# Attention scores from float32 queries and keys, four heads side by side in 32-row groups, in place of bf16 part sums over 96 rows

## What is computed

```python
mod = (silu(c) @ wmod)                     # six rows of 256 per batch: sa, ca, ga, sb, cb, gb
h = layernorm(x) * (1 + ca) + sa
q, k, v = (h @ Wq.T), (h @ Wk.T), (h @ Wv.T)      # 16 heads of 16 dimensions
q, k = rope(q), rope(k)
scores = einsum('bhqd,bhkd->bhqk', q, k) * 16**-0.5     # causal
attn = softmax(scores)
x = x + ga * ((attn @ v) @ Wo.T)
h = layernorm(x) * (1 + cb) + sb
x = x + gb * soft_moe(h)    # 8 experts of 128 slots: dispatch and combine softmax, gelu
```

## Time and profile before

| what | value |
|---|---|
| median of 3 runs | 3296.63 us (3295.2 to 3301.05) |
| the profiled execution: its own time, its span | 3297.0 us, 3295.2 us |
| TensorE matmul busy | 3071.7 us (93% of the span) |
| VectorE busy | 2252.1 us (68%) |
| ScalarE busy | 1763.6 us (54%) |
| GpSimd busy | 329.8 us (10%) |
| attention of batch 0 (first to last weighing) | from 162.6 us to 607 us |

### The profile page before, as it was taken

The page is one execution under the profiler, slowest core; times in us unless marked ns, Lnnn a source line. Parts: engine busy times, 40 slices in busy tenths (PEclk is TensorE's granted clock), DMA queues, the critical chain, the costliest instruction groups (busy, mean ns, idle before and its releaser), DMA issues.

```text
span 3295.2 us, 45435 instructions
## 1 busy us (share of the span) xinstructions
PE 3071.7 (93%) x17679; PEld 1544.8 (47%) x17679; DVE 2252.1 (68%) x4403; ACT 1763.6 (54%) x3199; POOL 329.8 (10%) x193
## 2 busy tenths in 40 slices
PE   5799999999889999998989999999997999999899
PEld 2433334447553333453854333344575433334468
DVE  4788887562678888756368888856546888885632
ACT  2366666564236666645514666654540566665560
POOL 3200000210400000111130000012122000002200
PEclk9799999999999999999999999999999999999999
DMA  4322201015502220002542202000443220100052
GB/s 129 99 40 40 40 2 39 14 52 197 149 20 40 40 40 27 20 7 95 190 119 46 39 9 40 27 20 7 151 163 103 40 41 11 31 27 27 9 179 81
DMA packets 123555, 201.89 MB, mean 61 GB/s; under 512 B 10094, under 2 KB 106996, under 8 KB 120232
## 3 DMA queue, kind: packets, MB, share of 16 engines
q1 hardware_dynamic: 110820, 148.58, 13.9%
q10 hardware_dynamic: 12520, 50.40, 8.2%
HBM read 156.01 MB, written 42.16 MB: 60 GB/s over the span
## 4 chain that ended last, share of the span: by engine, by line
PE 74%; DVE 17%; ACT 4%; issue 2%; POOL 1%; DMA 1%; ACTq 0%; SPq 0%; DVEq 0%; POOLq 0%
PE ps L694 14%; DVE pm L1269 12%; PE ps L674 10%; PE ps L614 9%; PE ps L795 7%; PE ps L850 7%; PE ps L627 6%; PE ps L881 3%; PE ps L870 3%; PE ps L574 2%; PE ps L738 2%; PE ps L659 2%; PE ps L678 1%; PE ps L808 1%; PE ps L603 1%
## 5 line engine op out<-in xcount | busy, mean ns | idle before, releaser
L1269 DVE TENSOR_REDUCE pm<-ps 128x1 f32<-128x512 f32 (+4 forms) x2560 | 1376.9, 602 | 273.6 <-PE ps L614 181.9
L983 ACT ACTIVATE R<-ps 128x512 f32<-128x512 f32 (+1 forms) x2240 | 1175.5, 593 | 603.0 <-PE ps L674 412.1
L674 PE MATMUL ps<-R 99*128 99x512 bf16 (+3 forms) x2560 | 827.9, 349 | 10.7 <-ACT R L983 6.0
L614 PE MATMUL ps<-R 96*128 96x512 bf16 x1536 | 578.6, 387 | 46.2 <-DVE pm L1269 40.7
L694 PE MATMUL ps<-R 128*17 128x512 f32 (+3 forms) x5120 | 528.9, 531 | 0.0
L614 PEld LDWEIGHTS ps<-R 96*128 96x128 bf16 x1536 | 147.3, 97 | 446.4 <-DVE pm L1269 372.0
L674 PEld LDWEIGHTS ps<-R 99*128 99x128 bf16 x2560 | 241.4, 97 | 146.0 <-ACT R L983 64.1
L694 PEld LDWEIGHTS ps<-R 128*17 128x17 f32 x5120 | 117.8, 96 | 280.1 <-issue 168.3
L850 PE MATMUL ps<-R 128*128 128x512 f32 x512 | 231.7, 610 | 14.0 <-ACT R L1050 13.9
L627 PE MATMUL ps<-R 128*128 128x257 f32 x1024 | 237.4, 388 | 4.1 <-ACT R L934 3.6
L795 PE MATMUL ps<-snT,R 128*128 128x512 f32 x512 | 230.1, 593 | 0.0
(11 more groups left out here) (151 smaller groups left out, 3321.7 us busy)
## 6 DMA issues: line engine op xcount, KB each, us to landing
R<-in_L_ffn_w_dram SPq DMA_DIRECT2D x64, 1024.0 KB, 5.8
R<-q_parts ACTq DMA_DIRECT2D x12, 768.0 KB
R<-k_parts ACTq DMA_DIRECT2D x12, 768.0 KB
R<-in_L_attn_x_dram SPq DMA_DIRECT2D x16, 512.0 KB, 8.4
q_parts<-R SPq DMA_DIRECT2D x16, 512.0 KB, 3.6
k_parts<-R SPq DMA_DIRECT2D x16, 512.0 KB, 3.4
R<-in_L_attn_x_dram SPq DMA_DIRECT2D x4, 2048.0 KB, 8.3
x_park<-R SPq DMA_DIRECT2D x16, 512.0 KB, 2.6
```

What stands on the lines that cost most here:

```text
L614: last = mm(ps[:, bank, :], qt(4 * c + r), kt(4 * kc, 4), start=True, stop=True)
L674: last = mm(bank[:, i * w:(i + 1) * w], kst[g % 2][0:BROWS, h0 + i, j * P:(j + 1) * P], qst[g % 2][0:BROWS, h0 + i, (c + 1) * CH - w:(c + ...
L983: A(Eb[s % ESLOTS][:, h0:h0 + n, 0:w], ps[:, u % NST, 0:n * w].rearrange("p (n w) -> p n w", n=n), ACT.Exp, scale=SCALE).then_inc(s_ex, 1)
L1269: mx = lambda o, i: V.tensor_reduce(o, i, AX.X, ALU.max)
```

## The change

Queries and keys stay float32. After the rotation they are parked as they are, 16 rows each, and `load_group` brings each head of a group to its own 32 partitions: head h has its 16 rows at 32h, and row 32h+16 holds ones for keys and the negated maximum for queries. All four groups have their own place in SBUF (`kg`, `qg`). A score matmul runs over 17 rows, a matmul of maxima over 16, in the 32-row group of its head, in float32. The three-part splitting on ScalarE, VectorE and GpSimd goes, as do the four instructions that split the negated maxima; `nrow` has two buffers.

The narrow tiles change: the last two tiles of a chunk (256 and 128 columns) form one step, with one unit per head; in a step at the diagonal the mask matmuls of two units (all 128 rows, 128 or 256 columns) follow behind the second of them. A chunk has 4c+3 steps; a batch has 144 steps and 576 units. The blocks of maxima are "diag", "near" (two matmuls of 256 columns), "edge" (two of 128) and "full", in number 592 as before, and they go round the heads in the order 2, 3, 0, 1 in place of all blocks of one head first. Steps are weighed 4 units behind instead of 3.

```diff
 def steps_of_chunk(k):
-    return 4 * (k % NC) + 4
+    c = k % NC
+    return [(j,) for j in range(4 * c + 2)] + [(4 * c + 2, 4 * c + 3)]
...
+UNITS = [(s, h) for s in range(NSTEP) for h in range(HG)]
...
+    blocks = [("diag", 0, 0), ("near", 0, 0), ("edge", 0, 0)]
+    blocks += [("full", r, kc) for kc in range(c) for r in range(4)]
+    for kind, r, kc in blocks:
+        for h in (2, 3, 0, 1):
+            yield k, h, kind, r, kc
...
-WEIGH_BEHIND, EVAC_BEHIND, TURN_BEHIND, GATHER_BEHIND = 3, 5, 8, 9
+WEIGH_BEHIND, EVAC_BEHIND, TURN_BEHIND, GATHER_BEHIND = 4, 5, 8, 9
...
-        kst = [view(R1, 8192 * i, 4096, bf16).rearrange("p (h t) -> p h t", h=HG) for i in range(2)]
-        qst = [view(R1, 8192 * i + 4096, 4096, bf16).rearrange("p (h t) -> p h t", h=HG) for i in range(2)]
+        kg = [view(R1, 4096 * g, 2048) for g in range(NG)]
+        qg = [view(R1, 4096 * g + 2048, 2048) for g in range(NG)]
...
+            for h in range(HG):
+                rows = slice(32 * h, 32 * h + HD)
+                eng.dma_start(kg[g][rows, tokens], k_park[:, HG * g + h, tokens]).then_inc(loaded, 16)
+                eng.dma_start(qg[g][rows, tokens], q_park[:, HG * g + h, tokens]).then_inc(loaded, 16)
+            eng.dma_start(kg[g][HD:P:32, tokens], ones_park[:, tokens]).then_inc(loaded, 16)
...
                 def qt(i):
-                    return qst[g % 2][0:KROWS, h, i * P:(i + 1) * P]
+                    return qg[g][32 * h:32 * h + KROWS, i * P:(i + 1) * P]
...
                 elif kind == "diag":
-                    mm(ps[:, bank, :], identb[:, :], maskb[:, :, :].rearrange("p r t -> p (r t)"),
-                       start=True, stop=True)
+                    mm(ps[:, bank, :], identb[:, :], maskq[:, :, :].rearrange("p r t -> p (r t)"),
+                       start=True, stop=True, skip_group_check=True)
...
+                elif kind == "near":
+                    mm(ps[:, bank, 0:2 * P], qt(4 * c + 2), kt(4 * c, 2), start=True, stop=True)
+                    last = mm(ps[:, bank, 2 * P:4 * P], qt(4 * c + 3), kt(4 * c, 2), start=True, stop=True)
+                elif kind == "edge":
                     mm(ps[:, bank, 0:P], qt(4 * c + 1), kt(4 * c, 1), start=True, stop=True)
-                    last = mm(ps[:, bank, P:4 * P], qt(4 * c + 3), kt(4 * c, 3), start=True, stop=True)
-                elif kind == "even":
-                    last = mm(ps[:, bank, 0:2 * P], qt(4 * c + 2), kt(4 * c, 2), start=True, stop=True)
+                    last = mm(ps[:, bank, P:2 * P], qt(4 * c + 3), kt(4 * c + 2, 1), start=True, stop=True)
...
                 def score_unit(u):
...
+                    rows = slice(32 * h, 32 * h + BROWS)
+                    for j, at, w in tiles_of_step(s):
+                        last = mm(ps[:, u % NST, at:at + w], kg[g][rows, j * P:(j + 1) * P],
+                                  qg[g][rows, (c + 1) * CH - w:(c + 1) * CH], start=at == 0, stop=True, skip_group_check=True)
+                    if not diagonal(s):
+                        last.then_inc(s_st, 1)
+                    elif h % 2:
+                        mask_units(u - 1, u)
+
+                def mask_units(*pair):
+                    for u in pair:
+                        s, h = UNITS[u]
+                        n = len(tiles_of_step(s))
+                        bank = ps[:, u % NST, :].rearrange("p (n w) -> p n w", n=2)
+                        mm(bank[:, 0:n, 0:P], identb[:, :], maskk[:, 0:n, :],
+                           start=False, stop=True, skip_group_check=True).then_inc(s_st, 1)
...
-            def parts(b, i):
-
-                qk = i % 2
-                act.wait_ge(s_rr, b * QU + i + 1)
-                nc.scalar.copy(rope_part[set_of(b, i)][qk], rope_out[set_of(b, i)]).then_inc(s_p0, 1)
-                act.wait_ge(s_r2, b * QU + i + 1)
-                nc.scalar.copy(rope_part[set_of(b, i)][1 - qk], rope_out[set_of(b, i)]).then_inc(s_p1, 1)
...
-            def remainder(b, i):
-                dve.wait_ge(s_p0, b * QU + i + 1)
-                V.tensor_tensor(out=rope_out[set_of(b, i)], in0=rope_out[set_of(b, i)], in1=rope_part[set_of(b, i)][i % 2],
-                                op=ALU.subtract).then_inc(s_r2, 1)
...
-                V.tensor_reduce(negm[:, :, :], pm[:, k % 2, :, :, 0:2 + k % NC], AX.X, ALU.max, negate=True).then_inc(s_own_nm, 1)
...
-                V.tensor_tensor(out=negp[:, :, 2, :], in0=negr[:, :, :], in1=negp[:, :, 1, :], op=ALU.subtract).then_inc(s_nm, 1)
+                V.tensor_reduce(negm[:, :, :], pm[:, k % 2, :, :, 0:3 + k % NC], AX.X, ALU.max, negate=True).then_inc(s_nm, 1)
```

More of the change, by code:

```diff
@@ L40, in steps_of_chunk, with tiles_of_step, step_width @@
 def steps_of_chunk(k):
-    return 4 * (k % NC) + 4
-STEPS = [(k, j) for k in range(NK) for j in range(steps_of_chunk(k))]
+    c = k % NC
+    return [(j,) for j in range(4 * c + 2)] + [(4 * c + 2, 4 * c + 3)]
+STEPS = [(k, js) for k in range(NK) for js in steps_of_chunk(k)]
 NSTEP = len(STEPS)
-FIRST_STEP = [STEPS.index((k, 0)) for k in range(NK)]
-LAST_STEP = [FIRST_STEP[k] + steps_of_chunk(k) - 1 for k in range(NK)]
-def diagonal(s):
[L53 to L62, removed]
+FIRST_STEP = [[k for k, js in STEPS].index(c) for c in range(NK)]
+LAST_STEP = [FIRST_STEP[k] + len(steps_of_chunk(k)) - 1 for k in range(NK)]
+def tiles_of_step(s):
+    k, js = STEPS[s]
+    out, at = [], 0
+    for j in js:
+        w = CH - max(j - 4 * (k % NC), 0) * P
+        out.append((j, at, w))
+        at += w
+    return out
+def step_width(s):
+    return sum(w for j, at, w in tiles_of_step(s))
+def diagonal(s):
+    k, js = STEPS[s]
+    return js[0] >= 4 * (k % NC)
+UNITS = [(s, h) for s in range(NSTEP) for h in range(HG)]
 SU = len(UNITS)
-FIRST_UNIT = [[u[0] for u in UNITS].index(s) for s in range(NSTEP)]
-LAST_UNIT = [FIRST_UNIT[s + 1] - 1 if s + 1 < NSTEP else SU - 1 for s in range(NSTEP)]
+FIRST_UNIT = [HG * s for s in range(NSTEP)]
+LAST_UNIT = [HG * s + HG - 1 for s in range(NSTEP)]
 def max_units_of_chunk(k):
     c = k % NC
[L71 to L77, removed]
+    blocks = [("diag", 0, 0), ("near", 0, 0), ("edge", 0, 0)]
[3 more added lines that the diff above has]
+            yield k, h, kind, r, kc
 ROWS_BEHIND = 4
@@ L139 @@
 LAST_UNIT_OF_CHUNK = [LAST_UNIT[LAST_STEP[k]] for k in range(NK)]
-WEIGH_AFTER = after_units([LAST_UNIT[s | 1] for s in range(NSTEP)], WEIGH_BEHIND)
+WEIGHED = [pair for k in range(NK) for pair in
+           [(s, s + 1) for s in range(FIRST_STEP[k], LAST_STEP[k], 2)] + [(LAST_STEP[k],)]]
+WEIGH_AFTER = after_units([LAST_UNIT[pair[-1]] for pair in WEIGHED], WEIGH_BEHIND)
 EVAC_AFTER = after_units(LAST_UNIT_OF_CHUNK, EVAC_BEHIND)
@@ L335, in adaln_block @@
         s_rr = sem("roped_ready")
[L336 to L339, removed]
[L340 removed]
+        s_pk = [sem(f"roped_parked{i}") for i in range(RSETS)]
         s_ldf = [sem(f"first_group_loaded{c}") for c in range(NC)]
@@ L670, in score_unit @@
                     if u >= NST:
                         pe.wait_ge(s_ex, b * SU + (u + 1 - NST))
-                    bank = ps[:, u % NST, :]
-                    for i in range(n):
-                        last = mm(bank[:, i * w:(i + 1) * w], kst[g % 2][0:BROWS, h0 + i, j * P:(j + 1) * P],
-                                  qst[g % 2][0:BROWS, h0 + i, (c + 1) * CH - w:(c + 1) * CH],
-                                  start=i == 0, stop=True, skip_group_check=True)
-                    if diagonal(s) >= 0:
-                        last = mm(bank[:, 0:n * w].rearrange("p (n w) -> p n w", n=n)[:, :, 0:P], identb[:, :],
-                                  maskTb[:, 0:n, :], start=False, stop=True, skip_group_check=True)
@@ L779, in _ @@
                         beside(BESIDE_AT.index(u))
-                for s in range(NSTEP):
-                    if LAST_UNIT[s | 1] + WEIGH_BEHIND >= SU:
-                        weigh(s)
+                for pair in WEIGHED:
+                    if LAST_UNIT[pair[-1]] + WEIGH_BEHIND >= SU:
+                        for s in pair:
+                            weigh(s)
                 def logits(n):
@@ L947, in _ @@
                 modulated(0, c)
-            for i in range(QU):
-                parts(0, i)
             act.wait_ge(s_pt, 3)
@@ L1093, in _ @@
                         modulated(b + 1, c)
[L1094 to L1102 removed]
+                for c in range(NC):
+                    store(c)
         @block.gpsimd
```

187 lines of the change are left out of this document (61 added, 126 removed).

## The result

| | before | after |
|---|---|---|
| median of 4 runs | 3298.23 us (3295.2 to 3301.05) | 5818.98 us (5810.76 to 5820.14) |
| ratio of after to before, 95% interval | | 1.7638 [1.7607, 1.7668] |
| span of the profiled execution | 3295.2 us | 5808.9 us |
| mean granted clock of TensorE over the span | 0.981 | 0.689 |
| forecast | | 3790 us, range 3500 to 4180 |

What follows compares the result with a forecast made beforehand. Attention was taken as bound by TensorE's stream, VectorE close behind, and after the change by latency of the bank rings. Attention +464, maxima outside +70 and savings -39 gave +495 on 3297.0 us: 3790 us, range 3500 to 4180.

Steps and rivals of the forecast that it cites:

- a rival of 3%: Attention: no overlap of row groups, 16.1 us a pair, about 6150 us; a waits-lowered clock between 4480 and 6150; chance 3%.
- 464: All four attentions: 116 us more per batch, a group of heads taking 143 us instead of 112.2.
- The "diag" blocks: Attention: mask 0.2 us, switching 0.2 and lost overlap, about 0.6 us per block, 2.0 us per chunk.
- the bank turn: Attention: a bank is free again after 1.71 us (scores) or 1.80 us (maxima), so one per 0.57 or 0.60 us.
- a full pair: Attention, weighing to weighing: 7.15 us against 6.18 seen before, bounds 6.6 and 8.0; 12 pairs per group.
- the pair at the diagonal: Attention, once per chunk: masks over all rows let matmuls in flight leave first, weighing ending at 8.6 us.
- in program order, two at a time: Rival in attention: starts 0.43 us apart, a full pair 9.4 us, a diagonal 18.3, 4480 us in all; chance 7%.
- The narrow step: Attention, the step of two narrow tiles: masks at 0.96 and 2.9 us, weighing 0.65, 3.7 us together.
- The alignment of heads: Full pairs: in about a third of units, maxima share the unit's row group, pairs at up to 0.86 us; bound 8.0.
- +70 - 39: Maxima outside attention +70 us (boundaries 3 x 14, values 4 x 4, prologue 12); savings, mainly from dropped splitting, -39 us.
- The saving in the prologue: Start of the kernel: without splitting, the first maxima no longer wait for subtractions and masks, -15 us.
- the two slow ones: Rivals: starts 0.43 us apart, 4480 us, chance 7%; no overlap of row groups, about 6150 us, chance 3%.

Runs made afterwards that it cites:

- experiment 1: Kernel before with its bf16 score matmuls and maxima over 16 rows instead of 99 and 96: 4362.65 us.
- experiment 3, padded kernel: Kernel after with each head's row group filled up to 32 rows with zeros, result unchanged: 4834.86 us.
- experiment 4: Kernel after with groups filled to 32 rows, but each score matmul and maxima matmul over all 128 rows, so none overlap: 5874.44 us.
- experiment 5: Kernel after with groups filled to 32 rows by zeros, the mask matmul of the "diag" maxima left out: 4416.36 us.
- experiment 6: Kernel after with groups filled to 32 rows by zeros, maxima going round the heads as 0, 1, 2, 3 instead of 2, 3, 0, 1: 5382.24 us.

## Why the prediction was wrong, step by step

**The step that failed is the clock.** Every duration of the sum for attention was taken at full clock, because all of attention stood at 1.00 before, and a fall was named only within a rival of 3% (together with no overlap at all), and then only for waits. But waits did not grow: TensorE's wait for reductions was 52.8 us in the first attention, and it is busy 1064.88 of 1068 us. The clock fell because the matmuls use 16 and 17 rows, in a stage that had used 96 and 99. That it can do this by itself is shown by experiment 1 (+1068 us in the kernel before), and that it did so here by experiment 3 (-984 us for zero rows). An estimate of its share, from the mean clocks of the four attentions: 3357 of their 4163 us passed at half clock, and a full clock could give back at most half of that, 1678 us. The attentions were forecast at 1779 + 464 = 2243 us and took 1920 more, so at least some 240 us of that is something else.

The Trainium skill ("TensorE: Matmul & The Clock Gate", "What's actually happening") makes the clock depend on how busy the engine has been. The trace speaks against busyness alone: TensorE is busy 99% of the attention with 16 rows and of that with 128 (experiment 4), and the clock is at 0.60 in the one and at 1.00 in the other. Only the gap in experiment 3 fits it.

**The "diag" blocks, forecast at 0.6 us each.** The term took the mask at 0.2 us, the switching at 0.2, and what others would have overlapped at the rest. The padded kernel shows a block and a unit in 1.93 us even at full clock, where the two should have taken 0.6 more than the 0.6 of a pair's pace: 1.2. The switch from the mask (0.32 us), five of the eight narrow parts in one row group (5 x 0.11 us) and one float32 unit up to the next mask (1.05 us) follow one another, with only the last three narrow parts beside the unit. That all heads' "diag" blocks now come one after another, where they came one per head before, puts four such gaps together. How the 205.1 us of a padded group (327.03 to 532.14, from the weighings) divides against the 144.6 that the forecast's terms give with all 16 of its "diag" blocks inside:

| part of the group | forecast | padded kernel | the same steps in experiment 5 |
|---|---|---|---|
| 2 pairs and 2 narrow steps with four "diag" blocks each | 31.3 us | 61.8 us | 38.7 us |
| 7 steps behind these or near them, in the padded kernel at a clock of 0.50 to 0.89 | 49.5 us | 74.9 us | 67.2 us |
| 9 steps at full clock there: pairs 7.3 to 8.5, diagonals 8.55, one narrow step 4.59 | 63.8 us | 68.5 us | 69.8 us |

So the "diag" mask makes most of the first row's excess, but only the smaller part of the second's. With it gone, a pair with four "diag" blocks is 8.55 us instead of 18.2, and the clock stays at 1.00 in it. Of the 25 us that the second row has too much, 8 are the load of experiment 3, for which TensorE of the kernel after doesn't stop; the rest is time at the low clock that I can't put down to one thing. The kernel after has its own low clock on top: its group takes about 254 us.

**What held.** Four row groups at once, by starts within 0.02 us; the bank turn of 1.80 us and so a block and a unit per 0.60 us (0.60 measured); a full pair 7.15 us (7.30 in the padded kernel at full clock, 15.8 without overlap against the rival's 16.1); the pair at the diagonal 8.6 (8.55). The rival "in program order, two at a time" is out by the same rows: the second part of a matmul starts 0.53 us after its first (328.87 and 329.40), with three other matmuls started in between. The narrow step was 4.59 at full clock against 3.7. The alignment of heads, which I had at up to 0.86 us in a third of the units, shows at most as pairs of 7.72 us beside the 7.30, within my bound of 8.0; pairs of 8.25 and 8.50 us also hold matmuls over all rows (four diagonal masks, and the four instructions of line 710). As an edit by itself (experiment 6) the order is worth 547 us.

**Outside attention** I had +70 - 39 = +31 us; it was +129. The saving in the prologue came as forecast and a little more: the first block of maxima starts at 83.62 us instead of 104.19, 20.6 earlier against 15.

```profile
83.62 0.38 PE L595 MATMUL ps<-maskq,identb 128*128 128x512 bf16 x1 [3.30 <-issue]
```

But the blocks that follow do not take 12 us more. At 1.2 GHz the "diag" blocks set the pace, a reduction each 2.54 us (1.85 of waiting and 0.69 of work):

```profile
87.86 0.69 DVE L1231 TENSOR_REDUCE pm<-ps 128x4 f32<-128x512 f32 x1 [1.85 <-PE ps L598]
```

VectorE, the bound of this stretch before, is busy 12.59 us in the window from 105 to 128 instead of 22.18. The last of the 41 is done at about 132 us, 49 us for what took 24, and so the stage of the values begins 4 us later than before in spite of the early start (132.14 against 128.37). That stage with its maxima takes 7 us more (34.2 against 26.9), and the first units up to the first weighing 13 us more (20.7 against 7.4). So the first weighing came 24 us late instead of about as before, and the three boundaries cost 105 us instead of 30; in the padded kernel they cost 18 us each.

**The range** took in the forecast's own bounds and left out all rivals, and the two slow ones had 10% together. Its own terms were also added a little wrong: pairs and diagonals at their bounds give +66 and +189 us a batch instead of +55 and +194, so about 3590 to 4090 us instead of 3540 to 4100, which decides nothing here. The true fault lies before that: a resource that stood at its limit all through the trace, the clock, was taken as a constant although the change altered what it depends on.

## What to carry to other kernels

Cutting the rows of a matmul saved no time in it here (0.69 us at full clock with 17 rows and with 32), and where most of TensorE's stream was of this kind the clock stood at 1.2 GHz for 81% of attention with the engine hardly ever idle. When a change cuts the rows of the matmuls that fill a stage, put a half-clock case among the likely ones; read the granted clock per stage first, and try rows of zeros up to the full row group, which cost the matmuls nothing in time at the same clock (they gave 984 us here in float32 and 102 in bf16, although their loads cost some 100). Look at who issues the loads of such rows. And in a layout of row groups count each matmul over all rows as a barrier between row groups (418 us for 256 masks here), at the price of everything that would have run beside it, and keep masks within the row group that they belong to.

## What the runs showed of the hardware that was not expected

- The granted clock follows the rows that matmuls use. In the kernel before, scores and maxima over 16, 32, 64 and 96/99 rows gave 4363, 4264, 3473 and 3297 us, with 0.60, 0.64, 0.97 and 1.00 in the windows of the first attention.
- Rows of zeros count as rows: 5819 to 4835 us.
- A gap lowers the clock too: in the padded kernel TensorE waited 4.01 us and had 1.00 before and 0.52 in the 14 us behind. In the first attention of the kernel over 16 rows and of the kernel after, TensorE was never idle for 0.8 us, and the clock was low all the same.
- How rows side by side in row groups add up was not settled. Four groups of 17 rows, 68 in all, stood at 0.59, and one matmul of 64 rows at 0.97, while four groups of 32 kept 1.00 over successive pairs. But the first and the last are float32, with 512 columns in some 0.43 us, and the second is bf16, with 512 in 0.22 us, so the comparison changes two things at once.
- In row groups, a unit of another head starts ahead of the last narrow parts of the block before it in the program (748.81 against 748.91): starts are not strictly in program order. The Trainium skill ("TensorE: Matmul & The Clock Gate", section on packing small matmuls) says that they are; here the measurement decides. Yet experiment 6 shows that the freedom has an end: with neighbours in the same row group the same pair at full clock takes 9.51 us instead of 8.25.
- What splits the 418 us of experiment 5 between the barrier itself and the clock that it pulls down was not measured apart. The attentions make 380 of them (3236 to 2856 us), and time at half clock in them went from 1080 to 590 us; if all of that ran twice as fast at full clock, some 245 us would be the clock's and 135 the barrier's, an estimate.
